# A graph network on one core: one-hot banks built bit by bit, and a 512-column chunk moved from the end of each stream to its beginning

## The chip, the core and the metric

The kernel runs on one core of a Trainium2 chip. The metric is the device time of one execution in microseconds (us). The core has PE (matrix multiply), DVE (vector), ACT (scalar, with activation functions), POOL (here only the issuer of indirect DMAs, the gathers) and SP (only an issuer of DMAs). All have their own instruction stream and meet at semaphores.

## The reference

A graph network of four layers over 3125 nodes with 64 features and 103125 edges sorted by destination. In each layer, per edge, a message; per destination, a softmax-weighted sum of the messages:

```
msg   = relu(h[src] + edge_attr @ w + b) + 1e-7
m     = msg * t
ex    = exp(m - segment_max(m, dst)[dst])
agg   = segment_sum(msg * ex, dst) / (segment_sum(ex, dst) + 1e-16)
out   = relu(layernorm((h + agg) @ w1 + b1)) @ w2 + b2
```

Then a layer norm, a residual and the next layer. The edge product is the same in all layers; `h` changes.

## The kernel before

The edges are cut into two streams (the halves of the sorted list, the second one backwards), each of 51712 columns. Features of the first stream lie on partitions 0 to 63, of the second on 64 to 127. A stream is worked off in 54 chunks: 49 of 1024 columns, then 512, 512, 256, 128, 128 (`TAIL`). `width(c)` and `STARTS` give a chunk's columns.

For each chunk: PE multiplies the edge attributes into a PSUM tile X (L547); the rows `h[src]` are added. That happens in one of two ways. Either POOL gathers 128 rows with one indirect DMA (L504, table z_table to gath), and PE turns and adds them (L576). Or, for the second 512 columns of a *chosen* chunk, PE multiplies z_parts (h split in three bf16 parts) with a one-hot bank (L566, 150 matmuls: 25 node tiles, 3 parts, 2 streams). A gathered chunk of 1024 columns takes 16 gathers, a chosen one 8. Chunk 0 takes two fewer, since its first tile is empty. Chosen are the even chunks from 4 to 48 and those with c % 8 == 5, and in layers 1 to 3 also chunks 0 and 1. So chunks 4, 5, 6 and 12, 13, 14 and so on are three chosen ones in a row.

ACT then makes the message and its product with t (L684, L686), after the penalty from the keep bytes (L674, keep, which says whether two neighbours have the same destination; loaded for two chunks at a time by SP, L364). DVE works on each chunk in this order: running maximum (L936, L938, L941, L943), the numerator scan of the chunk before with its two transposes (L924, L969, L924), and, when ACT has the exponents, the denominator scan and the product (L953, L956). SP stores the rows (L374) to rows_table. A gather slot (3) comes free when PE has added the chunk, a PSUM tile (4) when the numerator scan is done.

The banks are built in layer 0. `bits_dram` has for each column one byte in each of five rows (rows by i, where the node's 128-block is 5 i + k, and the byte is the bit 4 << k if the row is the column's, else 0) and a sixth row with the lane in the block. SP broadcasts them to 128 partitions (`load_bits`). ACT finds where the lane is the partition's own (L708) and makes from it five lane patterns, one for each bit (L713, uint8). DVE builds the bank by five ANDs of 1280 int32 words (L1033), each of all five patterns with one row of bits, in two parts of two and three ANDs after the chunk's sums (`build_part`). SP stores each part to one_hot_dram; ACT's queue loads them again in layers 1 to 3 (L739), into one_hot and between in turn. In layer 0 a bank is built two chunks ahead of its use; those of chunks 0 and 1 are built in slots 50 and 52.

In chunks 1 to 25 of layer 0 POOL also gathers a row of sorted keys per chunk (L486), and after chunk 26 DVE finds the positions and centres the weights. Between layers stand the row gathers (L519) and the node work, at whose end z is stored for the next layer's gathers and split for PE (`split_z`, L994 to L998).

## Time and profile before

| | us |
|---|---|
| median of 3 runs | 3414.15 (3410.12 to 3417.74) |
| the profiled execution | 3407.53 |
| its span in the profile | 3405.7 |
| layer 0: first chunk on DVE to last rows turned | 54.4 to 928.2 |
| layer 1, the same | 1019.8 to 1728.2 |
| layer 1, chunks 4 and 5 begun | 1076.9 and 1094.9 |
| layer 2, first and last chunk begun | 1819.3 and 2521.3 |
| layer 3, first and last chunk begun | 2620.0 and 3322.2 |

Times are from one profiled execution, counted from the start of its span. A row of a timeline has the start, the duration, the engine, the line of the kernel, the operation, the tiles and shapes and, in brackets, the idle time before it and what ended it. The DVE instruction at L936 is the first of a chunk: the time of the n-th one in a layer is the start of that chunk.

### The profile page before, as it was taken

Reading aid. Unit: us, or ns where it says so; the run is one execution under the profiler, and the core shown is the slowest. Engines: PE = TensorE matmul, PEld = TensorE weight load, DVE = VectorE, ACT = ScalarE, POOL = GpSimd, SP = SyncE. Lnnn points to the kernel's source line nnn. Section 1 sums busy time; section 2 is a strip of 40 time slices with the busy share of each in tenths; the row PEclk is TensorE's granted clock in tenths of the full one; section 3 lists DMA queues with packets and bytes.
Section 4 is the critical chain, followed back from the end, with each engine's and each line's share of the span. In section 5 each row is a group of like instructions: output and inputs, shape, how many; then the busy total and the mean of one; then the engine's idle time right before and its main releaser. Section 6 shows DMA issues by size and latency. Waiting matters only on the chain.

```text
span 3405.7 us, 55091 instructions
## 1 busy us (share of the span) xinstructions
PE 2695.8 (79%) x21852; PEld 1361.5 (40%) x21852; DVE 2874.5 (84%) x2835; ACT 1782.3 (52%) x2240; POOL 2310.8 (68%) x2381
## 2 busy tenths in 40 slices
PE   2778877888279888988748899889938988899854
PEld 1334333334144444444333444444415444444423
DVE  6899999999857888898976888888875889888895
ACT  2777775666424544455443544545543445444554
POOL 5777776676257777777627777777735777777742
PEclk9889988889669999999858999999957999999975
DMA  5999999999838999999847999999964999999971
GB/s 147 282 273 311 304 289 259 272 289 287 231 117 269 287 304 302 295 295 297 215 122 219 305 292 306 283 298 309 276 154 136 294 292 294 305 298 300 280 187 39
DMA packets 1047266, 878.26 MB, mean 258 GB/s; under 512 B 911066, under 2 KB 937183, under 8 KB 1015200
## 3 DMA queue, kind: packets, MB, share of 16 engines
q1 hardware_dynamic: 940912, 478.76, 54.8%
q10 hardware_dynamic: 28960, 305.28, 23.8%
q0 software_dynamic: 77136, 90.71, 10.2%
q8 instruction: 171, 2.80, 0.3%
q14 instruction: 87, 0.71, 0.1%
HBM read 555.79 MB, written 318.70 MB: 257 GB/s over the span
## 4 chain that ended last, share of the span: by engine, by line
DVE 34%; PE 16%; SPq 15%; issue 9%; POOL 9%; DMA 8%; ACT 8%; DVEq 0%; ACTq 0%; POOLq 0%
PE X L566 13%; SPq L374 9%; POOL gath L504 8%; DVE decay L938 7%; DMA keep<-keep_dram 6%; DVE state_all L969 6%; DVE one_hot L1033 5%; DVE rows_all L924 4%; SPq L364 4%; DVE X L943 4%; DVE state_all L953 3%; ACT X L686 2%; ACT msg L684 2%; SPq L353 1%; PE X L547 1%
## 5 line engine op out<-in xcount | busy, mean ns | idle before, releaser
L504 POOL DMA_INDIRECT gath<-z_table,idx x2248 | 2189.6, 974 | 862.5 <-issue 694.3
L566 PE MATMUL X<-one_hot,z_parts 128*64 128x512 fp8e5 x11550 | 1352.1, 396 | 149.2 <-DVE one_hot L1033 124.5
L566 PEld LDWEIGHTS X<-one_hot,z_parts 128*64 128x64 bf16 x11550 | 666.9, 114 | 870.8 <-DVE one_hot L1033 162.3
L566 PE MATMUL X<-between,z_parts 128*64 128x512 fp8e5 x6750 | 763.2, 386 | 2.8 <-DMA between<-one_hot_dram 2.8
L696 ACT ACTIVATE decay<-X 128x1024 f32<-128x1024 f32 (+2 forms) x216 | 209.3, 969 | 927.5 <-DVE X L943 923.2
L566 PEld LDWEIGHTS X<-between,z_parts 128*64 128x64 bf16 x6750 | 380.8, 112 | 394.6 <-issue 72.1
L924 DVE STREAM_TRANSPOSE rows_all<-state_all 128x1024 f32<-128x1024 f32 (+3 forms) x432 | 505.9, 1171 | 8.4 <-DMA rows_table<-rows_all 1.0
L547 PE MATMUL X<-attr,enc_edge 64*64 64x512 f32 (+1 forms) x1648 | 268.5, 703 | 306.8 <-DVE state_all L969 297.4
L953 DVE TENSOR_TENSOR_SCAN state_all<-decay,state_all,X 128x1024 f32<-128x1024 f32 (+2 forms) x216 | 468.2, 2168 | 20.0 <-ACT X L701 20.0
L938 DVE TENSOR_TENSOR_SCAN decay<-X,decay 128x1023 f32<-128x1023 f32 (+2 forms) x216 | 477.2, 2209 | 7.7
L969 DVE TENSOR_TENSOR_SCAN state_all<-decay,state_all,X 128x1024 f32<-128x1024 f32 (+2 forms) x216 | 468.1, 2167 | 0.0
L684 ACT ACTIVATE msg<-X,edge_bias 128x1024 f32<-128x1024 f32 (+2 forms) x216 | 226.1, 1047 | 278.2 <-PE X L576 278.2
L936 DVE TENSOR_TENSOR decay<-decay,top 128x1 f32<-128x1 f32 x216 | 34.2, 158 | 351.7 <-ACT X L686 338.0
L674 ACT ACTIVATE decay<-keep 128x1024 f32<-128x1024 uint8 (+2 forms) x216 | 213.7, 990 | 223.4 <-DMA keep<-keep_dram 223.4
L956 DVE SCALAR_TENSOR_TENSOR X<-msg,X 128x1024 f32<-128x1024 f32 (+2 forms) x216 | 250.4, 1159 | 7.5
L943 DVE TENSOR_TENSOR X<-X,decay 128x1024 f32<-128x1024 f32 (+2 forms) x216 | 250.0, 1157 | 0.0
L576 PE MATMUL X<-ident,gath 128*128 128x128 f32 x1128 | 180.9, 296 | 80.9 <-DMA gath<-z_table,idx 80.7
L686 ACT ACTIVATE X<-msg,tcol 128x1024 f32<-128x1024 f32 (+2 forms) x216 | 229.6, 1063 | 7.0
L519 POOL DMA_INDIRECT between<-rows_table,pos_i x100 | 95.0, 950 | 180.3 <-DMA rows_table<-ends_row 104.4
L699 ACT ACTIVATE decay<-decay 128x1024 f32<-128x1024 f32 (+2 forms) x216 | 213.1, 987 | 0.0
L697 ACT ACTIVATE X<-X 128x1024 f32<-128x1024 f32 (+2 forms) x216 | 208.1, 963 | 0.0
L701 ACT ACTIVATE X<-X 128x1024 f32<-128x1024 f32 (+2 forms) x216 | 207.1, 959 | 0.0
(160 smaller groups left out, 1458.0 us busy)
## 6 DMA issues: line engine op xcount, KB each, us to landing
rows_table<-rows_all SPq DMA_DIRECT2D x784, 256.0 KB
attr<-attr_t SPq DMA_DIRECT2D x196, 512.0 KB
one_hot<-one_hot_dram ACTq DMA_DIRECT2D x48, 1920.0 KB
between<-one_hot_dram ACTq DMA_DIRECT2D x45, 1920.0 KB
one_hot<-one_hot_dram ACTq DMA_DIRECT2D x48, 1280.0 KB
one_hot_dram<-one_hot SPq DMA_DIRECT2D x31, 1920.0 KB
between<-one_hot_dram ACTq DMA_DIRECT2D x45, 1280.0 KB
one_hot_dram<-one_hot SPq DMA_DIRECT2D x31, 1280.0 KB
```

What stands on the lines that cost most here:

```text
L374: sp.dma_start(rows_by_chunk[blk, a, :, b0:b0 + n, :], rows[g % 2][a * SQ:(a + 1) * SQ, 0:n].rearrange("i b q j -> i b (q j)")).then_inc(s ...
L504: pool.indirect_dma_start(out=gath[s][:, n * F:(n + 1) * F], out_offset=None, in_=z_table, in_offset=bass.IndirectOffsetOnAxis(ap=idx[:, c ...
L547: last = nc.tensor.matmul(X[g % XS][h * F:(h + 1) * F, b * BANK:b * BANK + w], enc_edge2[b * F:(b + 1) * F, :], attr[s][b * F:(b + 1) * F, ...
L566: last = nc.tensor.matmul(x[h * F:(h + 1) * F, BANK:CH], z_parts[:, i * GB + k, third, :], bank[:, i, k, h * BANK:(h + 1) * BANK], start=F ...
L684: nc.scalar.activation(msg[s][:, 0:w], X[g % XS][:, 0:w], ACT.Relu, bias=edge_bias[:, :]).then_inc(msg_ready, 1)
L686: nc.scalar.activation(X[g % XS][:, 0:w], msg[s][:, 0:w], ACT.Copy, scale=tcol[:, layer:layer + 1])\
L924: v.transpose(rows[g % 2][:, 0:w // SQ, q, :], state[g % 2][:, q, 0:w].rearrange("p (b j) -> p b j", j=SQ))\
L938: v.tensor_tensor_scan(out=m[:, 1:w], data0=x[:, 0:w - 1], data1=m[:, 1:w], initial=m[:, 0:1], op0=ALU.max, op1=ALU.add).then_inc(run_max, 1)
L943: v.tensor_tensor(x, x, m, ALU.subtract).then_inc(shifted, 1)
L953: v.tensor_tensor_scan(out=state[g % 2][:, 0, 0:w], data0=decay[s][:, 0:w], data1=X[g % XS][:, 0:w], initial=state[(g - 1) % 2][:, 0, befo ...
L956: v.scalar_tensor_tensor(out=X[g % XS][:, 0:w], in0=msg[s][:, 0:w], scalar=EPS_MSG, in1=X[g % XS][:, 0:w], op0=ALU.add, op1=ALU.mult).then ...
L969: v.tensor_tensor_scan(out=state[g % 2][:, 1, 0:w], data0=decay[s][:, 0:w], data1=X[g % XS][:, 0:w], initial=state[(g - 1) % 2][:, 1, befo ...
```

## The change

Two things. The chunks: the first is now 512 columns wide (`HEAD`), followed by 49 of 1024, then 512, 256, 128, 128. The number of chunks stays 54. Every choice moves by one: chosen are the odd chunks from 5 to 49 and those with c % 8 == 6, in layers 1 to 3 also chunks 1 and 2, whose banks are built in slots 51 and 53. The number of banks stays 31. Attributes are packed in one row block per chunk, and rows are stored by square and not by chunk.

The banks: a bank is laid out by bit first and block row second. ACT makes one pattern, 255 where the lane is the partition's own. DVE narrows the five rows of bits by one AND with it (1280 words, own_bits in the free x_sb), and builds each of the five bit planes by one AND of own_bits with a word per partition, 1280 words each; parts of two and three as before. A slot of bits is free when narrowed is done. PE goes through a bank by bit and then by block row.

```diff
-TAIL = [512, 512, 256, 128, 128]
-WIDTHS = [CH] * ((COLS - sum(TAIL)) // CH) + TAIL
+HEAD = [512]
+TAIL = [512, 256, 128, 128]
+WIDTHS = HEAD + [CH] * ((COLS - sum(HEAD + TAIL)) // CH) + TAIL
...
-PARTS = [(0, SPLIT), (SPLIT, PIECES_1H)]
+PARTS = [(0, SPLIT), (SPLIT, GB)]
...
-FIRST_CHOSEN = [c for c in range(NCH) if (c % 2 == 0 or c % 8 == 5) and 4 <= c <= 48]
-CHOSEN = [c for c in range(NCH) if c < 2 or (c % 2 == 0 or c % 8 == 5) and 4 <= c <= 48]
-BUILD_SLOT = {0: 50, 1: 52}
+FIRST_CHOSEN = [c for c in range(NCH) if (c % 2 == 1 or c % 8 == 6) and 5 <= c <= 49]
+CHOSEN = [1, 2] + FIRST_CHOSEN
+BUILD_SLOT = {1: 51, 2: 53}
...
-                    sp.wait_ge(built, (n - BIT_SLOTS + 1) * PIECES_1H)
+                    sp.wait_ge(narrowed, n - BIT_SLOTS + 1)
...
-                for i in range(*PARTS[part]):
+                for k in range(*PARTS[part]):
                     if layer == 0:
-                        pe.wait_ge(built, bank_of(c) * PIECES_1H + i + 1)
-                    for k in range(GB):
+                        pe.wait_ge(built, bank_of(c) * GB + k + 1)
+                    for i in range(PIECES_1H):
...
-            def spread_lanes(n, ks):
...
-                for k in ks:
-                    nc.scalar.activation(lane_bits[n % 2][:, k * BW:(k + 1) * BW].bitcast(u8), lane_miss, ACT.Relu,
-                                         bias=bit_value[:, k:k + 1], scale=-float(4 << k)).then_inc(spread, 1)
+            def find_lanes(n):
+                act.wait_ge(bits_landed[n % BIT_SLOTS], 16 * (n // BIT_SLOTS + 1))
+                if n > 0:
+                    act.wait_ge(spread, n)
+                nc.scalar.activation(lane_miss, lane_bytes[n % BIT_SLOTS], ACT.Abs, bias=lane_off[:, :]).then_inc(off_lane, 1)
+                act.wait_ge(off_lane, n + 1)
+                if n > 1:
+                    act.wait_ge(narrowed, n - 1)
+                nc.scalar.activation(own_lane[n % 2].bitcast(u8), lane_miss, ACT.Relu, bias=all_bits[:, :], scale=-255.0).then_inc(spread, 1)
...
                 if part == 0:
                     dve.wait_ge(bits_landed[n % BIT_SLOTS], 16 * (n // BIT_SLOTS + 1))
-                    dve.wait_ge(spread, GB * (n + 1))
+                    dve.wait_ge(spread, n + 1)
+                    if n > 0:
+                        dve.wait_ge(built, n * GB)
+                    v.tensor_tensor(own_bits.rearrange("p (i c) -> p i c", c=BW),
+                                    bits_words[n % BIT_SLOTS][:, 0:PIECES_1H * BW].rearrange("p (i c) -> p i c", c=BW),
+                                    own_lane[n % 2].unsqueeze(1).broadcast_to([P, PIECES_1H, BW]), ALU.bitwise_and).then_inc(narrowed, 1)
...
-                for i in range(a, b):
-                    v.tensor_tensor(one_hot[:, i].rearrange("p k c -> p (k c)").bitcast(i32).rearrange("p (k c) -> p k c", k=GB),
-                                    lane_bits[n % 2].rearrange("p (k c) -> p k c", k=GB),
-                                    bits_words[n % BIT_SLOTS][:, i * BW:(i + 1) * BW].unsqueeze(1).broadcast_to([P, GB, BW]), ALU.bitwise_and)\
-                        .then_inc(built, 1)
+                dve.wait_ge(narrowed, n + 1)
+                for k in range(a, b):
+                    v.tensor_scalar(one_hot[:, k].rearrange("p i c -> p (i c)").bitcast(i32), own_bits, bit_mask[:, k:k + 1], None,
+                                    ALU.bitwise_and).then_inc(built, 1)
```

## Rows read from the trace of the kernel before

**Rows 1.** The page's busy line: busy us, share of the span, instructions.

```profile
PE 2695.8 (79%) x21852; PEld 1361.5 (40%) x21852; DVE 2874.5 (84%) x2835; ACT 1782.3 (52%) x2240; POOL 2310.8 (68%) x2381
```

**Rows 2.** Busy time by stretch, layer 0, layer 1: length; busy PE, PEld, DVE, ACT, POOL; clock, DMA.

```profile
250.00:922.00 672.00, 502.55 (x4036) 241.46 (x4031) 657.28 (x535) 456.04 (x501) 451.26 (x431) 0.87 0.97 281
...
998.00:1720.00 722.00, 624.85 (x5326) 305.63 (x5326) 601.07 (x468) 353.17 (x367) 523.99 (x554) 0.93 0.96 277
```

**Rows 3.** Waits in layer 0, DVE's and POOL's: us in total, times, longest.

```profile
DVE decay L936 <- ACT X L686: 7.7, 6, 1.3
...
POOL gath L504 <- PE X L576: 55.7, 9, 12.8
```

**Rows 4.** Groups by line and shape: count, busy us, mean ns, idle before.

```profile
L713 ACT ACTIVATE between<-between,bit_value 128x1024 uint8<-128x1024 uint8 x80 | 86.3, 1137 | 1.7 <-DVE one_hot L1033 1.2
...
L1033 DVE TENSOR_TENSOR one_hot<-between 128x1280 int32<-128x1280 int32 x55 | 79.0, 1486 | 0.0
```

**Rows 5.** The same view, DVE operations with one tensor input.

```profile
L890 DVE TENSOR_SCALAR between<-msg,sign 128x808 f32<-128x808 int32 x1 | 0.6, 635 | 0.0
...
L1003 DVE TENSOR_SCALAR state_all<-state_all 128x248 int32<-128x248 int32 x1 | 0.3, 290 | 4.1 <-DMA state_all<-src_banks 4.1
```

**Rows 6.** DVE's timeline, a build of three ANDs: start, duration, line.

```profile
264.38 4.29 DVE L1033 TENSOR_TENSOR one_hot<-between 128x1280 int32<-128x1280 int32 x3
```

**Rows 7.** POOL's timeline at the same time.

```profile
263.60 0.94 POOL L504 DMA_INDIRECT gath<-z_table,idx  x1 [0.30 <-issue]
264.84 1.84 POOL L504 DMA_INDIRECT gath<-z_table,idx  x1 [0.30 <-issue]
266.99 1.09 POOL L504 DMA_INDIRECT gath<-z_table,idx  x1 [0.30 <-issue]
```

**Rows 8.** DVE's timeline before layer 0, a one-tensor operation beside a gather.

```profile
36.22 0.51 DVE L1013 TENSOR_SCALAR state_all<-state_all 128x248 f32<-128x248 f32 x1
```

**Rows 9.** POOL's timeline, the key gathers of chunks 3, 17 and 25.

```profile
108.91 1.10 POOL L486 DMA_INDIRECT between<-keys_dram,row_i  x1 [0.30 <-issue]
...
332.39 1.85 POOL L486 DMA_INDIRECT between<-keys_dram,row_i  x1 [0.30 <-issue]
...
462.46 0.95 POOL L486 DMA_INDIRECT between<-keys_dram,row_i  x1 [0.30 <-issue]
```

**Rows 10.** DVE's timeline, layer 0: starts of chunks 3, 13, 21, 27, 48; its last.

```profile
115.71 0.16 DVE L936 TENSOR_TENSOR decay<-decay,top 128x1 f32<-128x1 f32 x1 [3.71 <-ACT X L686]
...
287.59 0.15 DVE L936 TENSOR_TENSOR decay<-decay,top 128x1 f32<-128x1 f32 x1
...
422.66 0.15 DVE L936 TENSOR_TENSOR decay<-decay,top 128x1 f32<-128x1 f32 x1
...
530.61 0.16 DVE L936 TENSOR_TENSOR decay<-decay,top 128x1 f32<-128x1 f32 x1
...
873.51 0.15 DVE L936 TENSOR_TENSOR decay<-decay,top 128x1 f32<-128x1 f32 x1
...
927.90 0.28 DVE L1093 TENSOR_TENSOR ends_row<-ends_w 1x128 f32<-1x128 f32 x1
```

**Rows 11.** DVE's timeline, layer 1: starts of chunks 0 and 1.

```profile
1019.75 0.16 DVE L936 TENSOR_TENSOR decay<-decay,top 128x1 f32<-128x1 f32 x1 [21.70 <-ACT X L686]
...
1037.72 0.16 DVE L936 TENSOR_TENSOR decay<-decay,top 128x1 f32<-128x1 f32 x1 [3.35 <-issue]
```

**Rows 12.** POOL's timeline, the first gather of layer 1.

```profile
991.22 0.94 POOL L504 DMA_INDIRECT gath<-z_table,idx  x1 [27.58 <-DMA z_table<-z_sb]
```

**Rows 13.** PE's timeline, chunk 0 of layer 1 by its one-hot bank.

```profile
998.10 18.72 PE L566 MATMUL X<-one_hot,z_parts 128*64 128x512 fp8e5 x150 [7.71 <-DVE z_parts L998]
```

**Rows 14.** DVE's timeline, layer 1: starts of chunks 45, 50 and 51.

```profile
1649.17 0.16 DVE L936 TENSOR_TENSOR decay<-decay,top 128x1 f32<-128x1 f32 x1 [3.73 <-ACT X L686]
...
1708.17 0.15 DVE L936 TENSOR_TENSOR decay<-decay,top 128x1 f32<-128x1 f32 x1
...
1714.83 0.15 DVE L936 TENSOR_TENSOR decay<-decay,top 128x1 f32<-128x1 f32 x1
```

More of the change, by code:

```diff
@@ L94, in pieces_before @@
     past = len(FIRST_CHOSEN) + (layer - 1) * len(CHOSEN) if layer > 0 else 0
-    return PIECES_1H * (past + sum(k < c for k in chosen(layer)))
+    return GB * (past + sum(k < c for k in chosen(layer)))
 def hot_slot(c):
@@ L108, in gathered_tiles @@
     return BANK // P if c in chosen(layer) else tiles(c)
-def block_of(c):
-    return STARTS[c] // CH, STARTS[c] % CH
+ATTR_PARTS = [P if w > BANK else F for w in WIDTHS]
 def attr_place(c):
-    blk, at = block_of(c)
-    if width(c) == CH:
-        return blk * P, 0, P
-    return blk * P + at * HALVES // CH * F, at * HALVES % CH, F
+    return sum(ATTR_PARTS[:c]), 0, ATTR_PARTS[c]
 def keep_block(c):
@@ L220, in gnn_kernel @@
         agg = between[:, N_SHARED:N_SHARED + N_AGG].rearrange("p (t e) -> p t e", e=2 * F)
-        hot = [one_hot, between[:, 0:HOT_WORDS].bitcast(fp8).rearrange("p (i k c) -> p i k c", i=PIECES_1H, k=GB)]
+        hot = [one_hot, between[:, 0:HOT_WORDS].bitcast(fp8).rearrange("p (k i c) -> p k i c", i=PIECES_1H, k=GB)]
         def carve(at, n, inner):
@@ L368, in store_rows @@
                 g = layer * NCH + c
-                blk, at = block_of(c)
-                b0 = at // SQ
-                n = NSQ - b0 if layer == 0 and c == NCH - 1 else width(c) // SQ
+                b0 = STARTS[c] // SQ
+                n = NBLK * NSQ - b0 if layer == 0 and c == NCH - 1 else width(c) // SQ
                 sp.wait_ge(rows_ready, g + 1)
                 for a in parts:
-                    sp.dma_start(rows_by_chunk[blk, a, :, b0:b0 + n, :],
+                    sp.dma_start(rows_by_square[a, :, b0:b0 + n, :],
                                  rows[g % 2][a * SQ:(a + 1) * SQ, 0:n].rearrange("i b q j -> i b (q j)")).then_inc(stored[g % 2], 16)
@@ L566, in add_by_one_hot @@
                                 last = nc.tensor.matmul(x[h * F:(h + 1) * F, BANK:CH], z_parts[:, i * GB + k, third, :],
-                                                        bank[:, i, k, h * BANK:(h + 1) * BANK], start=False,
-                                                        stop=(i * GB + k == NT - 1 and third == 2))
+                                                        bank[:, k, i, h * BANK:(h + 1) * BANK], start=False,
+                                                        stop=(k == GB - 1 and i == PIECES_1H - 1 and third == 2))
                     last.then_inc(used, 1)
@@ L805, in _ @@
                     n = bank_built_for(c + 3)
-                    building = layer == 0 and n is not None
-                    if building:
-                        spread_lanes(n, range(0, 2))
+                    if layer == 0 and n is not None:
+                        find_lanes(n)
                     exponents(layer, c)
-                    if building:
-                        spread_lanes(n, range(2, GB))
                     if c < NCH - 1:
@@ L879, in _ @@
             for k in range(GB):
[L880 removed]
+                p.mark(v.memset(bit_mask[:, k:k + 1], (4 << k) * 0x01010101))
                 p.mark(v.memset(scale_of[:, :].rearrange("p (i k) -> p i k", k=GB)[:, :, k:k + 1], PART_SCALE[k]))
+            p.mark(v.memset(all_bits[:, :], 255.0))
             p.mark(v.memset(top[1][:, :], 0.0))
@@ L1218 @@
     src_s = chunked(streams(src, 0)).transpose(3, 1, 2, 0).reshape(P, NBLK * KT * HALVES)
-    src_b = np.stack([streams(src, 0)[:, c * CH + BANK:(c + 1) * CH] for c in BANKS]).reshape(P, SUB)
+    src_b = np.stack([streams(src, 0)[:, STARTS[c] + BANK:STARTS[c] + CH] for c in BANKS]).reshape(P, SUB)
     attr_h = streams(attr, 0)
-    attr_s = np.zeros((NBLK * P, CH), attr.dtype)
+    attr_s = np.zeros((sum(ATTR_PARTS), CH), attr.dtype)
     for c in range(NCH):
```

38 lines of the change are left out of this document (15 added, 23 removed).

## The prediction

> **What bounds the kernel now.** I read the busy line of the page first [rows 1]: DVE 84%, PE 79%, POOL 68%. No engine bounds all of it, so the next view is the busy time by stage [rows 2]. In layer 0 (250 to 922 us) DVE works 657 of 672 us. In layer 1, as in 2 and 3, DVE works 601 of 722 and PE 625; POOL shows 524, but each gather is followed by 0.30 us of issue [rows 7], so its 554 gathers fill 554 x 1.25 = 692 us. The waits say the same [rows 3]: in layer 0 DVE waits 7.7 us in all and POOL waits 55.7 us for PE. So DVE bounds layer 0; layers 1 to 3 run at the pace of the gathers, with PE and DVE only a little behind them.
>
> In layer 0 the pace is set by two things. Until chunk 25 POOL also gathers keys: from key gather 17 to 25, eight chunks, it needs 130 us [rows 9], while DVE needs 135 us from chunk 13 to 21 [rows 10]. POOL is nearly as slow as DVE there, and the reader should keep this: a faster DVE meets POOL after a few us. After chunk 26 there are no key gathers, and only DVE counts.
>
> **The change part by part.** *(1) Building the one-hot bank, DVE.* Now: five ANDs of two tensors, 1280 words, 1.49 us each, a start every 1.40 us (the burst of three is 4.29 us) [rows 4, 6]: 7.0 us a bank. After: one such AND plus five ANDs against one word per partition. The trace has no such AND of this size. The two-tensor AND costs 1.49 us or 1.40 by its starts, 1.1 ns a word. The nearest rows [rows 5]: 808 words against a per-partition scalar took 0.635 us, where 1.1 ns a word would give 0.88; 248 int32 words in a bitwise AND with a constant took 0.290. The step from 248 to 808 is 0.62 ns a word, and half of the two-tensor rate would be 0.54. So 1280 words cost 0.290 + 1032 x 0.54 = 0.85 to 0.635 + 472 x 0.62 = 0.93 us, and starts lie some 0.09 closer, as they do for the two-tensor AND: 0.76 to 0.84. A like instruction of 248 words beside a gather took 0.51 us where 0.29 is usual [rows 8], so I take the upper end, 0.85. The two-tensor AND now has a dependent behind it (a wait for its own end): 1.5. A bank then costs 1.5 + 5 x 0.85 = 5.75 us (bounds 1.5 + 5 x 0.76 = 5.3, and at the two-tensor rate 1.5 + 5 x 1.40 = 8.5). Saved per bank 1.25 us, 31 banks.
>
> *(2) The same, ACT.* The five Relu passes of 1.14 us per bank [rows 4] become one. ACT is not the bound, but for most of layer 0 it makes DVE idle 1.3 us in every second chunk before L936 (7.7 us after 250 us [rows 3], some 6 more before); this goes. Freed bit slots one step earlier save nothing: nothing waits for them.
>
> *(3) The gathers beside a build.* While a burst of ANDs runs, the first gather takes 1.84 instead of 0.94 us and the next 1.09 [rows 6, 7]: gather starts fall into step with the 1.40 us of the ANDs, as if each waited for the running AND to end. Per bank POOL loses (130 - 96 x 1.25) / 5 = 2 us today. With shorter ANDs the wait is for a shorter instruction; I take 1.5 us (0.5 to 2).
>
> *(4) Layer 0 with the 512-column chunk first.* "Chunk 4 after" is the work of "chunk 3 before" plus nothing, but 512 columns came ahead of it, with 8 more gathers. Step a: key gather 3 was at 108.9 and DVE began chunk 3 at 115.7, 7 us later [rows 9, 10]: gather-bound. After, 8 gathers and one key more: 108.9 + 9 x 1.25 = 120.2, less a little contention, 119.6; chunk 4 starts at 126.6: **+10.9**. Step b, to the start of chunk 28 (27 before, 530.6 [rows 10]): DVE alone would need 24 x 12 + 15 banks x 5.75 + 8 for the position work = 382 us. POOL needs, to chunk 26, 240 gathers and 22 keys x 1.25 + 13 x 1.5 = 347 us, which puts chunk 26 at 126.6 + 347 = 474 at the earliest; where three chosen chunks follow each other PE needs 18 us a chunk (in layer 1 chunk 5 starts 18.0 us after 4), which adds some 3: 477. Then 8 + 24 + 8.6 + 2: chunk 28 at 519. That is 392.5 against 414.9: **-22.4**. Step c, 21 chunks to the start of chunk 49 (48 before, 873.5 [rows 10]): before 342.9 = 252 + 13 x 7. After 252 + 13 x 5.75 + 3 (PE in the triples) = 329.8: **-13.1**. Gathers: 224 x 1.25 + 20 = 300, hidden. Step d, the tail: before 54.7 (873.5 to 928.2 [rows 10]). After: one chunk of 12, then 512, 256, 128, 128 with the two last banks, 45.3: **-9.4**, of which 6.7 is the chunk moved away. Sum for layer 0: 10.9 - 22.4 - 13.1 - 9.4 = **-34**.
>
> The two last builds now stand one chunk nearer the end, the last part behind the 256-column chunk. It waits for the store of the bank before it; the gap between those two builds stays 18 us as today. The store of that last part lands perhaps 4 us after the layer ends and holds ACT's queue, on which the first denominator step stands; that step waits for the row gathers, which begin only after the last rows are stored, and they cover it. If they did not, it would be 4 us.
>
> *(5) Layers 1 to 3 with the 512-column chunk first.* Today DVE is idle 21.7 us at the start of a layer: PE first multiplies all of chunk 0 with its one-hot bank (18.7 us) [rows 11, 13]. After, chunk 0 needs only 6 gathers, and DVE starts some 14 us earlier. But what is late next is POOL. To finish chunk k+1 after it must gather what it gathered for chunk k before and 8 tiles more (chunk 1 and 2 are chosen, but 6 gathers went to chunk 0): 8 x 1.25 = 10 us later from chunk 4 on. Against this stands the tail, shorter by one 512-column chunk: 1714.8 - 1708.2 = 6.7 us [rows 14]. With everything else alike a layer becomes 10 - 6.7 = 3.3 us longer. The bound below: chunk 45's gathers end at 991.2 + 3 + 502 x 1.25 = 1621 [rows 12] and DVE begins it at 1649.2 [rows 14], 28 us later, where the gathers alone would allow about 23 (gather of chunk 43 at 1601, 5 to land, twice 18 on PE, 2.4 on ACT, less what runs ahead). So 5 us of slack, and if the earlier start uses it, the layer is 2 us shorter. I take +2 for each layer, nearer to the bound above, because eight chunks take 107 to 112 us today and POOL's share is 88 x 1.25 = 110: **+6** in three layers (bounds -9 to +15). Nothing of the packing of attr, the row stores, or the bytes of a bank changes a size; I cost these at nothing, and DMA carries them in the same time.
>
> The sum: -34 + 6 = -28. The profiled execution, 3407.5, would become 3379.5. The runs' median is 6.6 above that execution, so I predict 3414.15 - 28 = **3386**.
>
> **The rivals.** *(A) The ANDs run at the two-tensor rate*, so the change doesn't do what it says. Then a bank costs 8.5 us. Step b: 288 + 15 x 8.5 + 8 = 424, +9; step c: 252 + 110.5 = 362.5, +20; tail -4; start +11; layers +6: +42, 3456. For it: no row has an int32 AND with a per-partition word. Against it: a per-partition scalar and a bitwise AND each ran at the faster rate in rows 5.
>
> *(B) The fast ANDs hold the gathers back, and it ends slower.* If a gather had to wait for the whole burst and not for the running instruction, POOL would lose 5.75 us per bank. To chunk 26 it then needs 327 + 13 x 5.75 = 402, chunk 28 starts at 569, +39 with step a; step c becomes 280 + 75 = 355, +12; tail -9; layers +6: +47, 3461. It turns from faster to slower at about 1.5 + 28 / 13 = 3.7 us lost per bank. For it: POOL already has only 5 us of room in eight chunks. Against it: the gather in rows 7 waits for one AND, not three. The Trainium skill speaks for this rival: "SBUF — State Buffer", section "Who interferes with whom", says that a DVE instruction in a two-port mode and a GpSimd instruction share a port pair which the first takes for its whole instruction while the other blocks. By that rule the sum would be this rival's 3461 if back-to-back ANDs never let go, and the forecast if they let go between two; no row before shows a long AND of that kind beside a gather.
>
> *(C) The head pays.* Gathers turn out to have slack, and each layer 1 to 3 keeps 3 us or more of its earlier start: -9 instead of +6, with cheaper ANDs (5.3 a bank, -6 in layer 0): 3365. For it: PE and DVE, not POOL, are named by most waits.
>
> *(D) The head costs.* The 512 columns come first, all else is 10 us late, and DVE waits for keep bytes in every even chunk, which are now the gathered ones: +5 per layer, and the gain in step b is half: 3386 + 9 + 11 = 3406.
>
> **How the numbers follow.** Forecast (3374 to 3397) 0.50; C 0.14; D 0.20; B 0.10; A 0.06. A measurement of this kernel tells about 0.2%, 7 us, from no change. Faster by more than that: forecast, C, and most of D: 0.79. Within: the rest of D and mild forms of B: 0.07. Slower: A and B: 0.14. The range takes in C and D: 3355 to 3412.
>
> **What would show it.** Right: in the profile after, an AND against a word at 0.83 to 0.95 us; DVE starts chunk 28 near 519 and chunk 49 near 849; layer 0's last rows turned near 894; gathers beside a build at most 1.9 us; DVE's idle time at the start of layer 1 split in two (a few us before chunk 0, some 18 before chunk 1), and chunks 5 to 49 of layers 1 to 3 about 10 us later, counted from the first gather, than their like before. Wrong: ANDs of 1.4 us (A), gathers of 3 us in layer 0 (B), or a layer 1 that is 5 us or more shorter from first gather to last row (C).

## The result and the profile after

The kernel after takes 3472.86 us (median of 4 runs, 3462.18 to 3483.57) against 3412.30 (4 runs, 3410.12 to 3417.74): a ratio of 1.017 [1.0143, 1.0198]. It is slower by 60 us; forecast were 3386 and a range of 3355 to 3412. The profiled execution has a span of 3481.7 us, before 3405.7: 76.0 us more.

The page of after, its busy line (it answers to [rows 1]) and the chain that ended last:

```profile
PE 2696.1 (77%) x21852; PEld 1358.7 (39%) x21852; DVE 2828.6 (81%) x2867; ACT 1654.9 (48%) x2116; POOL 2309.7 (66%) x2381
...
DVE 31%; SPq 22%; PE 11%; DMA 11%; issue 9%; POOL 9%; ACT 5%; DVEq 0%; ACTq 0%; POOLq 0%
SPq L372 14%; PE X L564 9%; DMA keep<-keep_dram 8%; POOL gath L502 8%; SPq L363 8%; DVE decay L930 7%; DVE state_all L961 7%; DVE rows_all L916 6%; DVE X L935 4%; DVE state_all L945 3%; ACT X L684 2%; ACT msg L682 2%; DVE one_hot L1031 1%; DVE between L1109 1%; DMA gath<-z_table,idx 1%
```

Every engine has less work or the same (DVE 46 us less), but for fractions of a us. What grew on the chain is SPq, the sync engine's queue (22%; it was 15%), and the transfer of the keep bytes (8%; it was 6%). L372 stores rows, L363 loads keep bytes.

Busy time by stretch, as in [rows 2] (length; PE, PEld, DVE, ACT, POOL; clock, DMA share, GB/s). The second stretch covers layer 1:

```profile
250.00:922.00 672.00, 508.14 (x4073) 244.43 (x4073) 622.88 (x571) 359.37 (x404) 451.38 (x432) 0.87 0.99 287
975.00:1740.00 765.00, 630.43 (x5338) 306.59 (x5332) 614.27 (x488) 355.68 (x378) 529.82 (x558) 0.90 0.93 265
```

The waits of layer 0, which answer to [rows 3]:

```profile
DVE decay L928 <- ACT X L684: 20.0, 9, 5.2
DVE one_hot L1031 <- DMA one_hot_dram<-one_hot: 5.0, 2, 3.4
...
POOL gath L502 <- PE X L574: 41.9, 11, 11.1
```

DVE is busy 34 us less in this stretch (622.9, it was 657.3) and now waits where it hardly waited before: 20.0 us for ACT (it was 7.7) and 5.0 us for the store of a bank.

DVE's timeline, first the build of one bank [rows 6], then the starts of chunks 4, 28, 49 and 53 [rows 10]:

```profile
527.94 2.47 DVE L1031 TENSOR_SCALAR one_hot<-x_sb,bit_mask 128x1280 int32<-128x1280 int32 x3
530.54 1.49 DVE L1022 TENSOR_TENSOR x_sb<-between 128x1280 int32<-128x1280 int32 x1
532.17 1.68 DVE L1031 TENSOR_SCALAR one_hot<-x_sb,bit_mask 128x1280 int32<-128x1280 int32 x2
...
127.69 0.16 DVE L928 TENSOR_TENSOR decay<-decay,top 128x1 f32<-128x1 f32 x1 [3.95 <-ACT X L684]
...
533.77 0.15 DVE L928 TENSOR_TENSOR decay<-decay,top 128x1 f32<-128x1 f32 x1
...
867.01 0.15 DVE L928 TENSOR_TENSOR decay<-decay,top 128x1 f32<-128x1 f32 x1
...
903.99 0.15 DVE L928 TENSOR_TENSOR decay<-decay,top 128x1 f32<-128x1 f32 x1
```

POOL beside that build [rows 7], with gathers of 1.38, 1.29, 2.34 and 1.19 us where 0.95 is usual:

```profile
527.55 1.38 POOL L502 DMA_INDIRECT gath<-z_table,idx  x1 [0.30 <-issue]
529.24 1.29 POOL L502 DMA_INDIRECT gath<-z_table,idx  x1 [0.31 <-issue]
530.83 2.34 POOL L502 DMA_INDIRECT gath<-z_table,idx  x1 [0.30 <-issue]
533.48 1.19 POOL L502 DMA_INDIRECT gath<-z_table,idx  x1 [0.30 <-issue]
534.97 0.95 POOL L502 DMA_INDIRECT gath<-z_table,idx  x1 [0.30 <-issue]
```

The head of layer 1, DVE's chunks 0 and 1 [rows 11]:

```profile
994.68 0.16 DVE L928 TENSOR_TENSOR decay<-decay,top 128x1 f32<-128x1 f32 x1 [10.35 <-ACT X L684]
1021.59 0.16 DVE L928 TENSOR_TENSOR decay<-decay,top 128x1 f32<-128x1 f32 x1 [17.19 <-issue]
```

**Where the time went.** I cut both traces at the start of chunk 53, the last chunk of a layer. Up to it in layer 0: 920.4 before, 904.0 after, 16.4 gained. From there to chunk 53 of layers 1, 2 and 3: 802.7, 798.2 and 800.9 before, 833.9, 825.7 and 834.4 after, 92.2 lost. Behind it 83.5 and 83.7. So all of the loss is in layers 1 to 3, which build no bank. Most of it lies in the middle of a layer, 25.6 of the 31 us of layer 1, and is spread evenly there: in the 40 chunks 6 to 45, after takes 12.0 us from the start of an even chunk to that of the odd one behind it and 17.1 us from there to the next even chunk; before these were 13.1 and 14.7. A pair was 27.8 us and is 29.1.

The chain of waits of before and of after from 1300 to 1400 us shows what a pair waits for (start, length, what). Before:

```profile
1340.36 1.25 DVE rows_all L924
...
1344.00 2.73 SPq L374
1346.77 3.71 SPq L364
1350.52 4.21 DMA keep<-keep_dram
...
1375.07 2.24 DVE state_all L969
...
1378.59 8.18 PE X L566 x60
```

After:

```profile
1344.55 4.90 DMA keep<-keep_dram
...
1352.90 2.36 DVE decay L930
...
1360.06 1.26 DVE rows_all L916
...
1363.69 4.48 SPq L372
...
1368.21 3.65 SPq L363
1371.90 4.27 DMA keep<-keep_dram
...
1392.22 7.58 SPq L363
1399.84 4.95 DMA keep<-keep_dram
```

It is a loop through four queues (ACT, DVE, the sync engine, and the DMA transfer itself). Keep bytes land; ACT makes the penalties and messages of the even chunk; DVE works 8.6 us on that chunk, and in it turns the rows of the chunk before; the sync engine stores those rows and only then loads the keep bytes of the next pair, since there are two buffers and this is where its queue comes to it. From landing to the first row store is 11.9 us here (1349.45 to 1361.33); the rest is how long the stores and the load take to issue and land. In the 40 chunks 6 to 45 of layer 1, which are 20 pairs, the chain goes through 18 keep loads after and through 10 before.

What sets the pace before is shown by POOL in these 40 chunks. First the stretch in the columns of [rows 2] and POOL's waits before, then its waits after:

```profile
1107.75:1663.42 555.67, 500.30 (x4308) 244.90 (x4304) 476.52 (x361) 278.77 (x280) 419.77 (x445) 0.95 1.01 296
POOL gath L504 <- issue: 134.2, 439, 0.7
POOL gath L504 <- PE X L576: 1.8, 6, 0.3
...
POOL gath L502 <- issue: 130.5, 427, 0.7
POOL gath L502 <- PE X L574: 30.1, 19, 8.3
```

"issue" is here the 0.30 us behind each gather. Before, the gathers and these gaps fill 419.8 + 134.2 = 554.0 of the 555.7 us: the middle of a layer runs at the pace of the gathers, 27.7 us a pair. After, they fill 551.3 of 581.3 us (busy 420.8, in the row further down), and POOL stands 30.1 us waiting for PE to free a gather slot: the loop, at 29.1 us a pair, has become slower than the gathers.

The sync engine's timeline and ACT's show what stands beside such a load. After (ACT's rows first):

```profile
1332.21 0.33 ACTq L734 DMA_DIRECT2D one_hot<-one_hot_dram  x1
...
1349.47 1.06 ACT L672 ACTIVATE decay<-keep 128x1024 f32<-128x1024 uint8 x1 [7.33 <-DMA keep<-keep_dram]
```

```profile
1331.05 11.80 SPq L372 DMA_DIRECT2D rows_table<-rows_all  x4
1342.89 2.72 SPq L363 DMA_DIRECT2D keep<-keep_dram  x2
```

The ACT load at 1332.21 belongs to chunk 23, an odd chosen one, and by the kernel's order is the larger part of a bank's reload. It goes out 1.2 us behind the first of the four row stores; these take 11.8 us to issue, and the keep load stands behind them. When they land, ACT has been idle 7.3 us for them. Before, the last reload ahead of the keep load of 1346.77 is the smaller part, issued at 1342.93 in chunk 23, and the four stores there take 5.1 us.

### The profile page after: what moved, and what is told of

Read it like the earlier page. It is cut to its first block, busy times and chain, and to the rows that moved or that the text cites. A ratio compares the mean times of both kernels' runs of the same rounds, so it can differ in the third digit from the quotient of the medians.

```text
span 3481.7 us, 55001 instructions
## 1 busy us (share of the span) xinstructions
PE 2696.1 (77%) x21852; PEld 1358.7 (39%) x21852; DVE 2828.6 (81%) x2867; ACT 1654.9 (48%) x2116; POOL 2309.7 (66%) x2381
## 4 chain that ended last, share of the span: by engine, by line
DVE 31%; SPq 22%; PE 11%; DMA 11%; issue 9%; POOL 9%; ACT 5%; DVEq 0%; ACTq 0%; POOLq 0%
SPq L372 14%; PE X L564 9%; DMA keep<-keep_dram 8%; POOL gath L502 8%; SPq L363 8%; DVE decay L930 7%; DVE state_all L961 7%; DVE rows_all L916 6%; DVE X L935 4%; DVE state_all L945 3%; ACT X L684 2%; ACT msg L682 2%; DVE one_hot L1031 1%; DVE between L1109 1%; DMA gath<-z_table,idx 1%
## 5 line engine op out<-in xcount | busy, mean ns | idle before, releaser
L930 DVE TENSOR_TENSOR_SCAN decay<-X,decay 128x1023 f32<-128x1023 f32 (+2 forms) x216 | 477.2, 2209 | 7.7
L672 ACT ACTIVATE decay<-keep 128x1024 f32<-128x1024 uint8 (+2 forms) x216 | 213.8, 990 | 396.6 <-DMA keep<-keep_dram 396.6
L545 PEld LDWEIGHTS X<-attr,enc_edge 64*64 64x64 f32 x1648 | 52.9, 149 | 439.1 <-issue 412.7
L574 PEld LDWEIGHTS X<-ident,gath 128*128 128x128 f32 x1128 | 127.6, 148 | 241.4 <-DMA gath<-z_table,idx 139.1
## 6 DMA issues: line engine op xcount, KB each, us to landing
one_hot_dram<-one_hot SPq DMA_DIRECT2D x31, 1920.0 KB, 10.7
```

The lines of the kernel that those rows point to most:

```text
L545: last = nc.tensor.matmul(X[g % XS][h * F:(h + 1) * F, b * BANK:b * BANK + w], enc_edge2[b * F:(b + 1) * F, :], attr[s][b * F:(b + 1) * F, ...
L574: last = nc.tensor.matmul(X[g % XS][:, k * P:(k + 1) * P], gath[s][:, k * P:(k + 1) * P], ident[:, :], is_transpose=True, start=False, sto ...
L930: v.tensor_tensor_scan(out=m[:, 1:w], data0=x[:, 0:w - 1], data1=m[:, 1:w], initial=m[:, 0:1], op0=ALU.max, op1=ALU.add).then_inc(run_max, 1)
```

## The experiments

Two theories of the loss. **T1:** the chosen chunks moved from even to odd, but a keep block is still a pair that begins with an even chunk. ACT reloads a bank in two parts: 1.31 MB in the chunk before the chosen one, as soon as PE has used the first two fifths of the old bank, and 1.97 MB in the chosen chunk itself. With odd chosen chunks the 1.97 MB part is issued just before the keep load, where 1.31 MB stood before, and the stores and keep load of the loop share the DMA engines with it. **T2:** the attribute load in the sync engine's queue waits for PE, which in a chosen chunk has 90 matmuls ahead; the stores and the keep load stand behind that wait. A third, **C** (not the rival C of the prediction), is about layer 0: the transfers, and not DVE, took the missing gain.

The table has the complete kernels on chips where the kernel before takes 3412 to 3419 us; g10 and g11 leave out part of the computation and follow below. "Layers" is the sum from chunk 53 of layer 0 to chunk 53 of layer 3; "keep waits" ACT's waits for keep bytes in the whole execution; the next column 40 chunks (6 to 45) of layer 1 with the DMA engines' busy share in them; the last the mean issue time of the row stores ahead of a keep load and of the load, from the sync engine's timeline, for the 23 or 24 keep loads that are issued between 1050 and 1720 us.

| kernel | median us | ratio to before | layers | keep waits | 40 chunks, share | stores + keep issue |
|---|---|---|---|---|---|---|
| before | 3412.3 | | 2401.8 | 223.4 | 555.7, 1.01 | 5.9 + 4.9 |
| after | 3472.9 | 1.017 [1.0143, 1.0198] | 2494.0 | 396.6 | 581.3, 0.98 | 7.2 + 5.4 |
| e1 building alone | 3398.8 | 0.9947 [0.9925, 0.9969] | 2419.1 | 259.4 | 562.1, 1.00 | 6.3 + 4.7 |
| e2 order alone | 3498.6 | 1.0223 [1.0191, 1.0255] | 2490.2 | 377.3 | 583.6, 0.97 | 7.1 + 5.7 |
| e3 after, pairs shifted | 3424.5 | 1.0016 [1.0001, 1.0031] | 2442.7 | 305.7 | 562.7, 1.00 | 6.0 + 6.1 |
| e4 after, reload late | 3397.4 | 0.9925 [0.9898, 0.9952] | 2411.2 | 258.3 | 555.9, 1.01 | 7.4 + 2.8 |
| e5 before, pairs shifted | 3474.0 | 1.0166 [1.0143, 1.019] | 2468.9 | 368.2 | 579.4, 0.97 | 6.8 + 5.1 |
| e6 after, attr late | 3491.2 | 1.0208 [1.019, 1.0227] | 2510.7 | 381.8 | 587.1, 0.97 | 6.5 + 5.7 |
| e7 after, 3 keep buffers | 3387.6 | 0.9916 [0.99, 0.9933] | 2402.9 | 3.9 | 553.6, 1.02 | 8.6 + 2.7 |
| e9 after, parts swapped | 3460.4 | 1.0133 [1.0107, 1.0159] | 2473.3 | 249.7 | 569.2, 1.00 | 6.1 + 3.8 |
| g13 before, 3 keep buffers | 3399.8 | 0.9942 [0.9923, 0.9962] | 2391.9 | 4.4 | 552.9, 1.01 | 6.8 + 3.3 |
| g8 building, 3 keep buffers | 3376.6 | 0.9872 [0.9854, 0.9889] | 2391.6 | 4.2 | 550.5, 1.02 | 7.9 + 2.3 |

The last column gives an estimate of the loop: 11.9 us from landing to the first store, the stores, the load, and its landing, 4.7 us in the mean of those on the chain of after and of e4 (5.0 in before). That is 29.2 us a pair after (measured 29.1), 27.7 before, just the pace of the gathers, and 26.8 in e4, below it. It does not rank all kernels: for e3 it gives 28.7 where 28.1 was measured, for e9 26.5 where it was 28.5.

**e1 and e2: one half of the change each.** e1 is the kernel after with the lines of `HEAD`, `TAIL`, `FIRST_CHOSEN`, `CHOSEN`, `BUILD_SLOT` and the packing of attr and rows put back; e2 is the kernel before with these lines alone.

> Half of the change: the kernel before with its own chunk order and chosen chunks, and the one-hot matrices built by bit (one AND that narrows, five ANDs with a constant word). If the loss sits in the order of the chunks (theory T1 or T2, below), layers 1 to 3 keep the 801 us of before from chunk 53 to chunk 53, and layer 0 shrinks by 15 to 35 us: 3375 to 3397 us. If the building itself had caused the loss (the ANDs starve GpSimd or the bank stores come later), layers 1 to 3, which build nothing, could not show it, and the time would come out above 3412 with all of the difference in layer 0.

> The other half: the building of before, and each stream begins with a 512-column chunk, so that the chosen chunks (whose one-hot matrices are reloaded) are mostly odd where they were mostly even. Both theories of the loss expect layers 1 to 3 at 826 to 834 us each from chunk 53 to chunk 53, as in the kernel after (before: 801), and so 3412 + 92, less some 10 of the tail and head: 3485 to 3505 us. If the loss needs both parts, this comes out under 3440.

Measured: e1 3398.8, e2 3498.6. The building gains 17.6 us against the 3416.4 of that chip and the order loses 82. In e1's profile layer 0 gives 27.7 us (chunk 53 at 892.7). Its layers are 806 us each and not the 801 expected, with 36 us more of keep waits; that is not the building, since with three keep buffers the layers agree (g8 and g13, 2391.6 and 2391.9). With two buffers the layers vary more: g11 below, which differs from before in layers 1 to 3 only in that it reloads the same bank each time, takes 2418.0. Why these two are slower than before is open.

**e3 and e5: the pairs shifted by one**, in the kernel after and, as a mirror, in the kernel before.

```diff
-    return min(c // KEEP_CHUNKS, NKEEP - 1)
+    return min((c + 1) // KEEP_CHUNKS, NKEEP - 1)
...
-                    if c % KEEP_CHUNKS == 0 and c // KEEP_CHUNKS < NKEEP - 1 and layer * NKEEP + c // KEEP_CHUNKS >= 1:
-                        load_keep(layer * NKEEP + c // KEEP_CHUNKS + KEEP_SLOTS - 1)
+                    if c == 0 and layer > 0:
+                        load_keep(layer * NKEEP + 1)
+                    if c % KEEP_CHUNKS == 1 and (c + 3) // KEEP_CHUNKS < NKEEP:
+                        load_keep(layer * NKEEP + (c + 3) // KEEP_CHUNKS)
```

> The kernel after with the pairs of chunks that one keep load serves shifted by one: {0}, {1,2}, {3,4} and so on, where they are {0,1}, {2,3}. Both T1 (the keep load for an even chunk goes out just behind the 1.97 MB part of a bank's reload, where before it went out behind the 1.31 MB part) and T2 (an attribute load that waits behind 90 matmuls of a chosen chunk stands ahead of the keep load in the sync engine's queue) are about which of the two chunks of a pair issues the keep load, and expect the old pairing of chosen chunk and keep load to be back: 801 to 808 us a layer, 3385 to 3400 us in all. If the order costs something that has nothing to do with the keep loads, it stays at 3460 to 3480.

> The mirror of e3: the kernel before, with the pairs of chunks that one keep load serves shifted by one, so that the keep load goes out in the odd chunks, behind the 1.97 MB part of the reload that the even chosen chunks issue. T1 and T2 expect the loss of the kernel after to appear in the kernel before: layers 1 to 3 at 815 to 834 us from chunk 53 to chunk 53 (before: 801), 3455 to 3510 us in all. If the keep load's place behind a reload is not what costs, it stays at 3405 to 3425.

Measured: e5 makes the kernel before, with nothing else touched, 56 us slower, and its layers take 824.0, 817.1 and 827.8. Its waits:

```profile
ACT decay L676 <- DMA keep<-keep_dram: 368.2, 68, 10.0
```

against 223.4 before. e3 takes back 51 of the 92 us in the layers, not all: 3424.5, above the 3400 expected. Both say that the loss hangs on which chunk of a pair carries the keep load. The mirror is not exact: e5 loses 67 us in the layers where after loses 92, and e3 leaves 41 of them. What these 41 are is open.

**e4: the 1.97 MB part one chunk later** (T1 against T2).

```diff
-                            k = c if part == 1 or c == 0 else c + 1
-                            if k in CHOSEN and k != 1 and CHOSEN.index(k) + HOT_SLOTS < len(CHOSEN):
-                                load_part(layer, CHOSEN.index(k) + HOT_SLOTS, part)
+                            ks = [k for k in (c - 1, c) if (k > 4 and k % 8 in (1, 3, 7)) == (k == c - 1)] if part == 1 else [c + (c > 0)]
+                            for k in ks:
+                                if k in CHOSEN and k != 1 and CHOSEN.index(k) + HOT_SLOTS < len(CHOSEN):
+                                    load_part(layer, CHOSEN.index(k) + HOT_SLOTS, part)
```

> The kernel after with the second (1.97 MB) part of a bank's reload issued one chunk later, so that it follows the keep load and does not stand before it. T1 expects most of the loss back: 805 to 812 us a layer, 3395 to 3420 us. T2 (the sync engine's queue is held by an attribute load's wait, whatever the banks' reloads do) expects no change: 826 to 834 us a layer, 3460 to 3480 us.

Measured: 3397.4; layers 807.1, 801.1, 803.0. 83 of the 92 us are back, and the place is where T1 has it: the keep load now issues in 2.8 us instead of 5.4, and the chain of the 40 chunks goes through 8 keep loads instead of 18. In the sync engine's timeline of e4:

```profile
1317.13 6.39 SPq L372 DMA_DIRECT2D rows_table<-rows_all  x4
1323.57 2.85 SPq L363 DMA_DIRECT2D keep<-keep_dram  x2
```

The Trainium skill, "DMA: Bandwidth & Descriptors", section "Queues, rings and completion order", says that a DMA engine takes turns between the queues that have work for it. By that rule a keep load would not stand behind the whole reload, but go at a share of the rate while the reload lasts. The shorter issue times of e4 agree; no run here shows the turns themselves.

**e6: the attribute load one chunk later** (T2).

```diff
-                    while loaded <= min(g + SLOTS + 2, (layer + 1) * NCH + SLOTS - 1, LAYERS * NCH - 1):
+                    while loaded <= min(g + SLOTS + 1, (layer + 1) * NCH + SLOTS - 1, LAYERS * NCH - 1):
```

> The kernel after with each attribute load issued one chunk later, so that its wait for 90 matmuls of a chosen chunk is over when the sync engine comes to it and the row stores and the keep load do not stand behind it. T2 expects most of the loss back: 3395 to 3430 us. T1 expects little: 3455 to 3480, keep loads as late as in the kernel after.

Measured: 3491.2, slower than after and above what either theory allowed. The edit did what it should: in the 40 chunks the sync engine waits 10.7 us for PE ahead of attribute loads, where it waited 24.4 in after. The keep waits stay all the same (381.8). By itself this run would leave a doubt, since PE now waits for attr. Its waits from 1100 to 1700 us:

```profile
ACT decay L672 <- DMA keep<-keep_dram: 120.8, 20, 8.9
...
PE X L545 <- DMA attr<-attr_t: 78.3, 15, 9.3
```

The other traces remove the doubt: that wait of the sync engine was 21.7 us in the 40 chunks of before, nearly what it is after, and 59.2 us in e4, which has the layers back. T2 falls as the cause.

**e7: a third keep buffer in the kernel after.**

```diff
-KEEP_SLOTS = 2
+KEEP_SLOTS = 3
...
-                    if c % KEEP_CHUNKS == 0 and c // KEEP_CHUNKS < NKEEP - 1 and layer * NKEEP + c // KEEP_CHUNKS >= 1:
+                    if c % KEEP_CHUNKS == 0 and c // KEEP_CHUNKS < NKEEP - 1 and 1 <= layer * NKEEP + c // KEEP_CHUNKS < LAYERS * NKEEP - KEEP_SLOTS + 1:
...
-                    load_keep((layer + 1) * NKEEP)
+                    load_keep((layer + 1) * NKEEP + KEEP_SLOTS - 2)
```

> The kernel after with three buffers for the keep values where it has two, so that each keep load is issued a pair of chunks (26 us) earlier and may land late without anyone waiting. If the whole loss of layers 1 to 3 is the wait of the penalties for keep, this gives 801 to 808 us a layer: 3385 to 3410 us. If what is short there is the transfer rate itself (DMA engines 96 to 98% busy in the 40 middle chunks of the kernel after), the waits move to the reloaded banks or the row stores and the layer stays above 815 us: over 3440.

Measured: 3387.6; layers 805.3, 797.3, 800.2; all keep waits of the execution in one row:

```profile
ACT decay L672 <- DMA keep<-keep_dram: 3.9, 1, 3.9
```

This cuts the loop and leaves everything else as in after, so the 91 us of the layers hung on the loop. The same 40 chunks of layer 1 in after and in e7:

```profile
1091.42:1672.71 581.29, 505.11 (x4302) 245.92 (x4300) 475.99 (x360) 278.32 (x280) 420.75 (x446) 0.92 0.98 284
```

```profile
1083.08:1636.63 553.55, 506.32 (x4293) 246.85 (x4291) 475.35 (x360) 278.48 (x280) 418.48 (x444) 0.95 1.02 299
```

What is left is the pace of the gathers. In e7 POOL's gathers and the gaps behind them fill 418.5 + 133.2 = 551.7 of 553.6 us, in e4 554.8 of 555.9, and in g13 and g8 below all but 2 us too; the chain of e7 goes through POOL for 222 of these us and through no keep load. The transfers run high as well, 296 to 299 GB/s for the same 165 MB at a share of 1.01 to 1.02. Whether that rate would be a second limit just behind the gathers, no run of layers 1 to 3 tells. But it need not be one to explain the times.

**e9: the two parts of a reload swapped in size** (`SPLIT = 3` instead of 2).

> The kernel after with the two parts of a bank's reload swapped in size (1.97 MB first, 1.31 MB second), so that the keep load of the even chunks stands behind 1.31 MB, as in the kernel before. T1 in its form of bytes (0.66 MB more ahead of the keep load is 2.2 us at 296 GB/s, some 22 times a layer) expects most of the loss back: 3395 to 3430 us. If it is the number or the moment of the parts and not their size, it stays at 3450 to 3480.

Measured: 3460.4. That is above the 3430 that T1 in its form of bytes allowed and in the range set for "the number or the moment of the parts". The keep waits did fall to e4's size (249.7), but the layers kept 71 of the 92 us. The chain that ended last has 30% in PE's matmuls with the banks (9% in after):

```profile
PE X L564 30%; SPq L372 8%; DVE decay L930 6%; DVE state_all L961 6%; POOL gath L502 5%; DMA keep<-keep_dram 4%; DVE rows_all L916 4%; SPq L363 3%; DVE X L935 3%; DVE state_all L945 2%; PE X L545 2%; ACT X L684 2%; ACT msg L682 2%; PE X L574 2%; DVE between L1109 1%
```

Two parts of this can be told apart in layer 1. In the 40 middle chunks e9 takes 569.2 us, 12 of the 25.6 us less than after. But its chunk 6 begins 192.9 us behind the chunk 53 before it, where after has 187.4: the new split costs 5.5 us at the head of a layer. So the size by itself brought back half of the loss in the middle, and the moment at which the second part goes out, which e4 moved, brought back nearly all of it (555.9 us). What keeps the other half in e9, and whether it is a new cost of the split, stays open.

**g8 and g13: three keep buffers with the building alone, and in the kernel before.** These two and the next two ran first as e8, e13, e10 and e11 on a chip where the kernel before took 4613 us (last section); the ratios there were 0.9936 [0.9907, 0.9965] for e8 and 0.9997 [0.9977, 1.0018] for e13, 0.9982 and 0.9999 for e10 and e11, and tell nothing of this question, since TensorE set the pace there. What was expected of e8 and e13 was:

> The new building with the chunk order of before, and three keep buffers. With the keep values never late, this against e7 (the same with the new order) prices the order alone: the prediction's head, tail and layer terms sum to 10.9 of step a, -9.4 of step d and +6 of the layers, about +7 us for the new order, so this would be 3375 to 3388 us. If the order still costs or brings something that is not the keep load, it differs from e7 by more than 10 us.

> The kernel before with three keep buffers alone. If the late keep loads are a cost in the kernel before too (223 us of waits for them), it falls below 3412; if the 40 middle chunks of a layer are held by the transfer rate instead (296 GB/s, DMA engines 101% busy in before; 299 to 301 GB/s in e7), only some 3 to 5 us a layer come back: 3398 to 3410 us. Against e7 (3387.6) it gives what the whole change is worth when no keep load is late: the prediction's sum says 28 us, its layer 0 terms without step b and c's shortfall some 15 to 20.

And of their second runs:

> e8 again, on another chip: there TensorE waited for its own instructions (705.6 us of it, 0.0 where these kernels took 3412) and everything ran a third longer, so it said nothing of the keep loads. As for e8: with the keep values never late, this against e7 prices the new order alone. The prediction's head, tail and layer terms sum to about +7 us for the new order, so this would be 3375 to 3388 us. If the order costs or brings something that is not the keep load, it differs from e7's 3387.6 by more than 10 us.

> e13 again, on another chip. The kernel before with three keep buffers alone. If the late keep loads cost in the kernel before too (223 us of waits for them), it falls well below 3412; if the 40 middle chunks of a layer are held by the transfer rate instead (296 GB/s, DMA engines 101% busy), only 3 to 5 us a layer come back: 3398 to 3410 us. Against e7 (3387.6) it gives what the whole change is worth when no keep load is late: the prediction's sum says 28 us.

Measured: g8 3376.6, g13 3399.8, both as expected. g8 is the fastest kernel here, 1.3% below before. Where no keep load is late the building is worth 23 us by the medians (3399.8 to 3376.6), 17 in the profiled executions, all of it in layer 0. The new order costs 11 us by the medians (3376.6 to 3387.6, on two chips; by the ratios 15). In the profiles it is 11.3 in the three layers (8.7, 1.9 and 0.6), but only 3.3 in all, because layer 0 is 8 us shorter in e7: g8 reaches chunk 53 at 904.4, e7 at 896.5 and e1, with two keep buffers, at 892.7. From 165 to 850 us DVE waits 22.1 us for the store of a bank in g8, 2.6 in e1. So 8 to 12 us may lie idle in the fastest kernel; no run tells why the stores are late there. The third buffer alone gives before 0.6%: its 223 us of keep waits were nearly all covered by the gathers that set its pace anyway.

**g10 and g11: layer 0 without the bank stores** (theory C), made from e4 and from before. They leave out part of the computation and are read in layer 0 alone (medians 3385.4 and 3423.4).

```diff
-                sp.dma_start(one_hot_dram[n * P:(n + 1) * P, a:b], one_hot[:, a:b]).then_inc(hot_stored[part], 16)
+                if n == 0:
+                    sp.dma_start(one_hot_dram[0:P, a:b], one_hot[:, a:b]).then_inc(hot_stored[part], 16)
+                else:
+                    sp.dma_start(one_hot_dram[n * P:(n + 1) * P, a:a + 1, 0:1, :], one_hot[:, a:a + 1, 0:1, :]).then_inc(hot_stored[part], 16)
...
-                n = bank_of(CHOSEN[j])
+                n = 0
```

> e10 again, on another chip. e4 without the bank stores of layer 0 (only bank 0 is stored in full, a strip of the others, and layers 1 to 3 reload bank 0's matrices in place of each bank's own): part of the computation is left out, and it is read in layer 0 alone. It takes 3.1 MB a bank off the DMA engines, which were 101% busy in the 40 middle chunks of layer 0 in e4. If the transfer rate holds layer 0 (theory C), these 40 chunks fall from 654 us to below 635, and the gain against g11 from the start of chunk 4 (3) to that of chunk 49 (48) comes to the predicted 30 to 37 us, where it was 21.5 with the stores. If VectorE and GpSimd hold it, they stay at 645 to 655.

> e11 again, on another chip. The kernel before without the bank stores of layer 0, part of the computation left out as in g10; read in layer 0 alone. With DMA engines 98% busy in its 40 middle chunks (673.8 us), theory C expects a smaller fall than in g10: to 655 to 668 us. If the new building's gain against it stays near 21 us as with the stores, the shortfall of the predicted 35 is not the transfers but the building's cover.

Measured, 40 chunks of layer 0, first g10, then g11:

```profile
163.62:809.39 645.77, 528.40 (x4294) 255.47 (x4292) 620.02 (x537) 374.42 (x411) 487.66 (x469) 0.91 0.81 181
```

```profile
168.46:842.28 673.82, 531.88 (x4284) 254.44 (x4282) 657.33 (x512) 476.68 (x510) 491.72 (x470) 0.89 0.77 174
```

g11 does not move (before: 673.8, DMA share 0.98), although I expected 655 to 668: before, DVE held layer 0 alone, 657 of 674 us. g10 falls from e4's 654.0 to 645.8, not below 635. From chunk 4 (3) to chunk 49 (48) the gain of the new building is 757.7 - 727.0 = 30.7 us without the stores, 26.6 in e7, 21.5 in e4 and 18.5 in after. The last two run the same instructions in layer 0, so 3 us are scatter. So C is half right at most: some 10 us of the gain are missing with two keep buffers and all stores, a third buffer brings back 5 to 8 of them with the stores in place, and 4 are left that came only without the stores.

## Why the prediction was wrong

**The step that failed is the last sentence of (5)**: "Nothing of the packing of attr, the row stores, or the bytes of a bank changes a size; I cost these at nothing, and DMA carries them in the same time." Sizes did stay: 878.3 MB in both. But the chosen chunks changed sides against the keep pairs, and the loads that the sync engine and ACT issue stood in another order. I never asked which reload a keep load would now follow. That is 92 us in the layers where 6 were forecast. What the runs put in its place is the loop above: 29.1 us a pair where the gathers need 27.7, with 397 us of waits for keep bytes (223 before), and e7 shows that without it the layers take 2402.9 us. That layers 1 to 3 run at the pace of the gathers, as I had read, was right as long as the loop was shorter. My own rows had a hint: the DMA share of 0.96 and 0.97 in [rows 2], of which I used only the engines' columns. So had the page of before: the sync engine's queue was 15% of the chain that ended last, and the transfer of keep bytes 6%.

**Step a** held: chunk 4 at 127.7, forecast 126.6. **Step b** did not: 406.1 us instead of 392.5. With the bank stores away it is 395.4 (g10), with three keep buffers 399.0 (e7). The four chunks from 20 to 24 took 72.4 us in after, 66.7 in g10 and 66.6 in e7; in after ACT waits 7.2 us for keep bytes there. So half of the 13.6 us is the keep bytes again, and the term itself was right to 3 us. **Step c**: 333.2 against 329.8, with 331.6 in g10: right to 3 us. **Step d**: 47.5 us (867.0 to 914.5) against 45.3; 3.7 of it is a wait for a row store. Sum for layer 0 to its last row: -13.7 instead of -34.

**(1) The cost of the ANDs** was right. The groups of after, in the view of [rows 4, 5]:

```profile
L1031 DVE TENSOR_SCALAR one_hot<-x_sb,bit_mask 128x1280 int32<-128x1280 int32 x155 | 129.1, 883 | 10.1 <-DMA one_hot_dram<-one_hot 5.0 <-PE X L564 1.3
L1022 DVE TENSOR_TENSOR x_sb<-between 128x1280 int32<-128x1280 int32 x21 | 31.3, 1492 | 1.1
```

883 ns each, forecast 0.83 to 0.95; a bank costs 2.47 + 1.49 + 1.68 = 5.64 us, forecast 5.75. **(2)** ACT works 127 us less; that DVE's short waits for it would go did not come true (20.0 us in the stretch of [rows 3] where there were 7.7). **(3)** was low: the five gather starts from 527.55 to 534.97 are 7.4 us where 5.0 are usual, so this bank costs POOL 2.4 us, not 1.5, and one gather took 2.34, more than the 1.9 that I allowed. In the mean it is less: the 468 gathers of the 40 chunks 6 to 45 of layer 0 are busy 487.3 us, in layer 1 446 are 420.8, which makes 46 us for 25 banks, an estimate of 1.8 each. **(5), the order**: counted from the first gather, chunk 5 after begins 95.9 us later and chunk 4 before 85.7, chunk 7 against 6 125.9 and 116.5: the 10 us of POOL are there. Without late keep loads a layer costs 3.8 us more in the mean (e7 against g8), where I took 2; single layers differ by 0.6 to 8.7. Two slips in the sums changed nothing: the terms of (5) give bounds of -6 to +10 for three layers, not -9 to +15, and those of rival B put chunk 28 at 571, not 569.

**The rivals.** A fell with the ANDs' 883 ns. B fell with the gathers of 1.2 to 2.3 us: 2.4 us for the bank shown, where it needed 3.7. The Trainium skill's rule that I named there ("SBUF — State Buffer", "Who interferes with whom") agrees with the trace if it is read for one instruction: the gather that began 0.4 us ahead of the burst of 2.47 us took 1.38 and ended inside the burst, as it would if the pair is let go between two ANDs. C was the wrong way. D named the thing that decided, the keep bytes waited for in even chunks, and gave it 5 us a layer; it was 31. I took its price from the 10 us by which everything is later, and not from the loop, in which the lateness of one keep load is passed on to the next: 1.3 us in each pair of the middle, 25.6 us in 20 pairs.

## What to carry to other kernels

A transfer that is small (here twice 128 KB) can set the pace if its buffer comes free in a loop through several queues. Write that loop out with every queue in it and compare its time with the pace of the engine that bounds the stage, before moving work between even and odd iterations: here they were 27.7 us and 27.7 us, and 1.4 us more in the loop cost 92 us. An order of issue can be a cost even if no byte changes, and the cure here was one more buffer for the transfer in the loop, not a faster engine. A wait that is in the profile of before costs nothing as long as something else is as slow; its 223 us there were worth 10, and the same wait at 397 us cost 90. And where every transfer is busy (a DMA share of 1.01), look at the engines before calling it the limit: the gathers explain the same time.

## What the runs showed of the hardware

On one chip all five kernels ran a third longer (before: 4613 us, 30 runs). The operations of DVE and POOL took what they take elsewhere (a gather 965 ns in the mean, a scan 2209). TensorE was longer at the same matmuls, at a mean granted clock of 0.793 (before, elsewhere: 0.876), and stood idle without a wait that the profile shows, which it calls issue. The group of the bank matmuls in e13 (the kernel before with three keep buffers) there:

```profile
L566 PE MATMUL X<-one_hot,z_parts 128*64 128x512 fp8e5 x11550 | 1660.0, 419 | 528.8 <-issue 453.6 <-DVE one_hot L1033 36.6 <-DVE z_parts L998 23.2
```

In the profile of before it has 1352.1 us busy and no idle time by issue. On that chip 61% of the chain was PE, and the third buffer was worth nothing (0.9997). Why TensorE was slower there is not known from these runs.
